# First expert layer of a two-layer attention and expert kernel: another order of the work around the routed tiles, a first batch that enters the feed-forward part in halves, a leaky step on GpSimd

## The reference, cut to what matters

```python
logits = (x @ wt.T + repeat(g @ wg.T)) / 2.0
scores = softmax(logits);  topk_w, topk_idx = top_k(scores, 2);  topk_w /= topk_w.sum(-1)
y_all  = (leaky(x @ w_gate[e]) * (x @ w_up[e])) @ w_down[e]        # only the chosen experts matter
p      = (leaky(x @ sw_gate) * (x @ sw_up)) @ sw_down              # leaky slope 0.01
y      = (y_all[topk_idx] * topk_w).sum(1) + p
# feed-forward part on y:
h = silu(y @ w1.T * s1) * (y @ w2.T * s2)
h = gelu(h @ h1.T * s);  h = gelu(h @ h2.T * s);  x = x + h @ w3.T * s3
```

## Time and profile before

| what | us |
|---|---|
| median of 3 runs | 2638.07 (2637.86 to 2645.0) |
| profiled execution, whole | 2652.06 |
| its span, first to last instruction | 2650.2 |
| TensorE busy in the span | 2507.8 (95%) |
| VectorE busy | 1417.1 (53%) |
| ScalarE busy | 1071.4 (40%) |
| GpSimd busy | 983.2 (37%) |
| mean granted TensorE clock | 0.967 of full |

### The profile page before, as it was taken

One profiled execution on the slowest core, in us unless ns is written; L12 is line 12 of the kernel. 1 busy time (PEld: TensorE's weight loads), 2 busy tenths in 40 slices (PEclk: granted clock), 3 DMA queues, 4 the chain that ended last, 5 costly groups with the idle time before them and its releaser, 6 DMA issues. The chain is left out here.

```text
span 2650.2 us, 37857 instructions
## 1 busy us (share of the span) xinstructions
PE 2507.8 (95%) x13266; PEld 1552.1 (59%) x13266; DVE 1417.1 (53%) x3288; ACT 1071.4 (40%) x2618; POOL 983.2 (37%) x1028
## 2 busy tenths in 40 slices
PE   7999999899999899699999999999999899899998
PEld 4565655534343467387878777556656567544456
DVE  7466575467667353432424243565565578455555
ACT  4767676344544223111111111465666355112122
POOL 3655465178768324531212121765655200000000
PEclk9999999989999889799999999999999999999997
DMA  4000000000000146300000100432333000400000
GB/s 160 1 1 1 1 1 21 9 13 13 13 13 9 39 129 198 125 1 1 1 0 1 43 1 1 146 123 77 106 114 98 0 1 1 131 1 3 3 10 26
DMA packets 91518, 108.52 MB, mean 41 GB/s; under 512 B 16396, under 2 KB 72597, under 8 KB 91078
## 3 DMA queue, kind: packets, MB, share of 16 engines
q1 hardware_dynamic: 87606, 96.27, 11.5%
q0 software_dynamic: 3728, 9.83, 1.3%
HBM read 92.52 MB, written 9.35 MB: 38 GB/s over the span
## 5 line engine op out<-in xcount | busy, mean ns | idle before, releaser
L1014 POOL TENSOR_TENSOR cb_sc<-cb_toep,cb_mk 128x128 f32<-128x128 f32 (+3 forms) x256 | 215.6, 870 | 190.7 <-ACT cb_pr L1052 180.1
L1014 POOL TENSOR_TENSOR cb_bias<-cb_bias,cb_mk 128x128 f32<-128x128 f32 (+3 forms) x256 | 215.3, 871 | 148.6 <-DMA cb_bias<-in_fside_16xSxS 148.5
L1653 DVE TENSOR_REDUCE gb_bmax<-PS 128x8 f32<-128x512 f32 x256 | 164.5, 685 | 87.0 <-PE PS L1431 86.6
L398 PE MATMUL PS<-ident,cb_pr 128*128 128x128 f32 x1280 | 198.6, 284 | 4.0 <-ACT cb_pr L1052 2.3
L699 DVE CUSTOM_DVE_ANT_0 cb_sc<-PS,cb_sc,cb_sneg 128x128 f32<-128x128 f32 (+3 forms) x256 | 129.9, 547 | 125.0 <-PE PS L388 121.5
L398 PEld LDWEIGHTS PS<-ident,cb_pr 128*128 128x128 f32 x1280 | 135.3, 141 | 96.9 <-issue 82.7
L1812 ACT ACTIVATE gb_pt<-PS 128x512 f32<-128x512 f32 x256 | 139.4, 596 | 111.0 <-PE PS L1438 105.8
L1058 ACT ACTIVATE cb_pt<-PS 128x128 f32<-128x128 f32 (+3 forms) x448 | 163.6, 414 | 39.1 <-PE PS L398 38.6
L1431 PE MATMUL PS<-gb_ks,gb_qs 32*128 32x512 f32 x512 | 171.6, 668 | 8.0 <-DVE gb_bmax L1653 6.4
L699 DVE CUSTOM_DVE_ANT_0 cb_bias<-PS,cb_bias,cb_sneg 128x128 f32<-128x128 f32 (+3 forms) x256 | 129.3, 546 | 90.2 <-PE PS L388 89.3
L2347 PE MATMUL PS<-eb_g,ff_h 128*128 128x256 f32 x768 | 175.4, 382 | 0.0
(11 more groups left out here) (652 smaller groups left out, 5039.2 us busy)
## 6 DMA issues: line engine op xcount, KB each, us to landing
cb_bias<-in_fside_16xSxS SPq DMA_DIRECT2D x64, 256.0 KB, 2.9
cb_bias<-in_fside_16xSxS SPq DMA_DIRECT2D x64, 192.0 KB, 2.5
ff_h<-in_L_ffn_h_w SPq DMA_DIRECT2D x2, 4096.0 KB, 15.6
cb_bias<-in_fside_16xSxS SPq DMA_DIRECT2D x64, 128.0 KB, 2.2
y_rows<-eb_g SPq DMA_DIRECT2D x19, 256.0 KB, 2.2
cb_toep<-rel_table SPq DMA_DIRECT2D x8, 512.0 KB, 7.4
cb_bias<-in_fside_16xSxS SPq DMA_DIRECT2D x64, 64.0 KB, 2.2
ff_w<-in_L_ffn_w_w SPq DMA_DIRECT2D x3, 1024.0 KB, 8.3
```

Source lines behind the costliest of these rows:

```text
L398: ins = pe.transpose(PS[:, bank, j * P:j * P + P], pr[:, v % 2, e, j * P:j * P + P], ident)
L1014: ins = pool.tensor_tensor(biases(v, e), turned(h, n) if L0 else biases(v, e), mk[:, b % 2, packed(t):packed(t) + n], ALU.add)
L1653: dve.tensor_reduce(bmax[:, n % 2, t, g + e, 0:NB], PS[:, bank + e, :].rearrange("p (n k) -> p n k", k=64), AX.X, ALU.max)\
```

## The change

In TensorE's order `into(0, 0)` and `into(0, 1)` move between the transposes and logits (and wait for 4 of the 5 shared weight loads; the fifth, `sw_down`, has the semaphore `mo_back`), `into(1, 1)` is split around `ranks`, and `turn_rows(1)` moves behind `pair_into(0)`. The ring `turned` has two banks instead of four, `logit` has banks 6 and 7. VectorE's order moves the products between the routing steps. Leaky of batches 0 to 2 becomes two ScalarE operations (0.01 x and 0.99 relu(x), both from PSUM) and an addition on GpSimd; batch 3 keeps the old form. The second multiplication of `hot_tiles` moves to GpSimd. Small dummy activations of Exp and Silu are added. There are two buffers `yg0` and `yg1` (batch 1 uses `yg1`, in h2's place); the gathers of a batch go by halves (tiles 0, 1 of both experts, then tiles 2, 3); batch 0 and 1 are gathered without a wait between, batch 2 waits for `mo_y` 1, batch 3 for `mo_y` 3 and stands behind the first group of weight sums. Batch 0 is combined, transposed and multiplied with w1 and w2 in two halves of 256 columns; `combine(1)` and `combine(2)` stand behind tiles 2 and 6 of the second half, `combine(3)` behind tile 1 of batch 1. S3 is made in two halves for each step. Cut to its core:

```diff
-        L, Hq, Hd = cut(2 * NJ, P, dtype=BF16), cut(2 * NJ, TILES, dtype=BF16), cut(2 * NJ, 2, TILES, dtype=BF16)
+        yg1, Hq, Hd = cut(YG, D), cut(2 * NJ, TILES, dtype=BF16), cut(2 * NJ, 2, TILES, dtype=BF16)
+        L = flat(yg1).bitcast(BF16).rearrange("p (k m) -> p k m", m=P)
...
+        yg = lambda b: yg1 if b == 1 else yg0
...
-            Turns(sm, uses, k) for k in ((0, 1, 6, 7), (4, 5), (0, 1), (2, 3), (4, 5), (6, 7), (6, 7), (6, 7)))
+            Turns(sm, uses, k) for k in ((0, 1), (6, 7), (0, 1), (2, 3), (4, 5), (6, 7), (6, 7), (6, 7)))
...
-                        pe.wait_ge(sm["mo_shared"], 16 * 5)
-                    for ring, name in ((gates, "gate"), (ups, "up")):
-                        bank = ring.put(pe, (name, b, e))
-                        for c in range(DC):
-                            ins = pe.matmul(PS[:, bank, :], sw[name][:, c, e, :], x_of(b)[:, c, :], start=(c == 0),
-                                            stop=(c == DC - 1))
-                        ins.then_inc(ring.filled((name, b, e)), 1)
+                        pe.wait_ge(sm["mo_shared"], 16 * 4)
+                    into_one(gates, "gate", b, e)
+                    into_one(ups, "up", b, e)
...
+                def turn_first_y(half):
+                    pe.wait_ge(sm["mo_y" if half else "mo_half"], 1)
+                    for c in range(DC):
+                        bank = turned_y.put(pe, (0, c, half))
+                        for e in range(2):
+                            ins = pe.transpose(PS[:, bank, e * P:e * P + P], yr[:, 2 * half + e, c * P:c * P + P], ident)
+                        ins.then_inc(turned_y.filled((0, c, half)), 1)
...
+                def first_hidden(half):
+                    for c in range(DC):
+                        turned_y.wait_emptied(pe, (0, c, half))
+                    if half == 0:
+                        pe.wait_ge(sm["ff_in"], 16 * 6)
+                    for m in range(FC):
+                        if half == 0 and m == 5:
+                            turn_first_y(1)
+                        for ring, name in ((gates, "w1"), (ups, "w2")):
+                            item = (name, 0, m) if half else (name, "half", m)
+                            bank = ring.put(pe, item)
+                            for c in range(DC):
+                                ins = pe.matmul(PS[:, bank, 0:HS], wf[name][:, c, m * P:m * P + P], yT[:, c, half * HS:half * HS + HS],
+                                                start=(c == 0), stop=(c == DC - 1))
+                            ins.then_inc(ring.filled(item), 1)
...
                 turn_x(1, 1)
                 logits(0)
+                into(0, 0)
                 turn_x(2, 0)
                 turn_x(2, 1)
                 logits(1)
+                into(0, 1)
                 turn_x(3, 0)
                 turn_x(3, 1)
                 logits(2)
                 logits(3)
...
-                into(0, 0)
-                into(0, 1)
                 into(1, 0)
                 down(0)
+                into_one(gates, "gate", 1, 1)
                 ranks()
-                into(1, 1)
+                into_one(ups, "up", 1, 1)
...
-                    if i + 1 < PAIRS:
+                    if 1 <= i and i + 1 < PAIRS:
                         turn_rows(i + 1)
                     if i < PAIRS:
                         pair_into(i)
+                    if i == 0:
+                        turn_rows(1)
...
-                turn_y(0)
-                for b in range(B):
+                turn_first_y(0)
+                first_hidden(0)
+                first_hidden(1)
+                feed_forward(0)
+                for b in range(1, B):
+                    hidden(b)
...
-                    link(dve.tensor_tensor(Hq, iota[:, 0:TILES].unsqueeze(1).to_broadcast([P, 2 * NJ, TILES]),
-                                           hi[:, :].unsqueeze(2).to_broadcast([P, 2 * NJ, TILES]), ALU.is_equal))
-                    dve.tensor_scalar(Hd[:, :, 0, :], Hq, own, None, ALU.mult)
-                    link(dve.tensor_tensor(Hd[:, :, 1, :], Hq, column.unsqueeze(2).to_broadcast([P, 2 * NJ, TILES]), ALU.mult))
+                    dve.tensor_tensor(Hq, iota[:, 0:TILES].unsqueeze(1).to_broadcast([P, 2 * NJ, TILES]),
+                                      hi[:, :].unsqueeze(2).to_broadcast([P, 2 * NJ, TILES]), ALU.is_equal).then_inc(sm["mo_tile_hot"], 1)
+                    dve.wait_ge(sm["mo_tile_hot"], 1)
+                    link(dve.tensor_scalar(Hd[:, :, 0, :], Hq, own, None, ALU.mult))
...
+                def gated_half(m, half):
+                    item = lambda name: (name, 0, m) if half else (name, "half", m)
+                    bank = ups.take(dve, item("w2"))
+                    gates.wait_emptied(dve, item("w1"))
+                    dve.scalar_tensor_tensor(out=g1[:, m, half * HS:half * HS + HS], in0=PS[:, bank, 0:HS],
+                                             scalar=wf["w2_s"][:, m:m + 1], in1=sa[:, m % 2, 0:HS], op0=ALU.mult,
+                                             op1=ALU.mult).then_inc(ups.emptied(item("w2")), 1)
...
                 copy_logits(1)
+                products(0, 0)
                 copy_x(3)
...
-                products(0, 1)
                 pick_second()
                 products(1, 0)
                 sums()
                 slots_of_tokens()
+                products(1, 1)
                 hot_tiles()
-                products(1, 1)
                 hot_slots(0)
                 hot_slots(1)
+                products(2, 0)
+                rows_of_slots()
+                products(2, 1)
                 experts_of_tiles()
-                products(2, 0)
-                products(2, 1)
-                rows_of_slots()
                 weights_of_tokens()
                 for i in range(PAIRS + 1):
                     if i < PAIRS:
                         pair_products(i)
                     if i:
                         copy_hidden(i - 1)
-                products(3, 0)
-                products(3, 1)
+                for e in range(2):
+                    leaky(3, e)
+                    products(3, e)
+                combine(0, (0, 1), "mo_half")
+                copy_first_y(0)
+                for m in range(FC):
+                    gated_half(m, 0)
+                    if m == 3:
+                        combine(0, (2, 3), "mo_y")
+                    elif m == 4:
+                        copy_first_y(1)
                 for b in range(B):
                     more = b + 1 < B
-                    if b == 0:
-                        ya.wait_emptied(dve, ("p", B - 1))
-                        yb.wait_emptied(dve, ("p", B - 1))
-                        combine(0)
-                        copy_y(0)
                     for m in range(FC):
-                        gated_rows(b, m)
+                        if b:
+                            gated_rows(b, m)
+                        else:
+                            gated_half(m, 1)
                         if m == 5:
                             first_sums(b, 1, 0)
                             third_sum(b, 1, 0)
-                        if b == 0 and m in (3, 4, 6):
-                            combine({3: 1, 4: 2, 6: 3}[m])
+                        if b == 0 and m == 2:
+                            combine(1, range(NT), "mo_y")
+                        elif b == 0 and m == 6:
+                            combine(2, range(NT), "mo_y")
+                        if b == 1 and m == 1:
+                            combine(3, range(NT), "mo_y")
...
+                        ups.wait_emptied(act, ("up", b - 1, e))
+                    if b < B - 1:
+                        act.activation(lk[:, e, :], PS[:, bank, :], ACT.Copy, scale=0.01)
+                        ins = act.activation(gs[:, e, :], PS[:, bank, :], ACT.Relu, scale=0.99)
+                    else:
+                        ins = act.activation(gs[:, e, :], PS[:, bank, :], ACT.Copy)
+                    ins.then_inc(gates.emptied(("gate", b, e)), 1)
 
...
+                act.activation(warm[:, 0:1], small["first"][:, 0:1], ACT.Exp, scale=0.0)
+                copy_x(0)
+                copy_x(1)
+                copy_x(2)
+                gate_copy(0, 0)
+                copy_x(3)
+                gate_copy(0, 1)
...
+                act.activation(warm[:, 1:2], small["first"][:, 0:1], ACT.Silu, scale=0.0)
...
+                def leaky(b, e):
+                    gates.wait_emptied(pool, ("gate", b, e))
+                    pool.tensor_tensor(lk[:, e, :], lk[:, e, :], gs[:, e, :], ALU.add).then_inc(sm["mo_lk"], 1)
+
+                def return_rows(b):
+                    if b > 1:
+                        pool.wait_ge(sm["mo_y"], b - 1 if b == 2 else b)
+                    for half in range(2):
+                        for k in range(2):
+                            for t in (2 * half, 2 * half + 1):
+                                n, at = k * NT + t, k * NJ + b * NT + t
```

(24 more changed lines are left out.)

89 lines of the change are left out of this document (55 added, 34 removed).

## The result

| | before | after |
|---|---|---|
| median of 13 runs each, us | 2641.41 (2637.26 to 2647.63) | 2626.19 (2616.93 to 2634.71) |
| ratio, 95% interval | | 0.9934 [0.9919, 0.9949] |
| profiled execution, us | 2652.06 | 2626.76 |
| mean granted clock | 0.967 | 0.976 |

The change makes the kernel 17.4 us faster by the ratio (0.66%; the interval is 13.5 to 21.4 us). I had forecast 23.5 us and 2614.6 us; the median lies 2.7 us above the end of my range. The two profiled executions differ by 25.3 us, more than the medians: the profile of before lies 10.7 us above its median, that of after 0.6 us above its own.

What follows compares the result with a forecast made beforehand. TensorE's waits and low clock ahead of 1160 us were taken as the loss. 20.5 us (second part) plus 3.0 (first part) make 23.5, from 2638.07 to 2614.6 us; own range 2609 to 2622, whole range 2600.5 to 2623.5.

Steps and rivals of the forecast that it cites:

- Part two: From the first returning gather to P5 of the first product: 84.4 us become 63.9, 20.5 us won (ends 18 to 25).
- T: Time of the first returning gather, 1046.86 us before the change, from which the feed-forward entry's steps are counted.
- Rival 1: Feed-forward entry: combine(1)'s sums are not held; 8.3 + 2.4 us more won, 2603.9 us; chance 0.18.
- rival 2: Feed-forward entry: DMA engines full with h1, first four gathers no sooner than all eight; 4.6 us less, 2619.2 us; chance 0.10.
- rival 4: Start: GpSimd multiplies element by element, delaying hot_slots and all gathers; at 35 us the time is 2646.7 us; chance 0.03.
- the collision: Second half: combine(1)'s sums held by GpSimd's weight sums; TensorE loses 8.3 us and 2.4 us of clock.
- T2's lead: First group's end: T2, behind combine(2), is ready about 3 us before P6's second half wants it, so costs nothing.
- Part one: Up to the first pair: reordered start brings gathers and pair loop earlier, 3.0 us won (ends minus 1.0 to 6).
- rival 3: Up to the first pair: clock stays low and GpSimd holds routing; minus 1.0 instead of plus 3.0, 2618.6 us; chance 0.08.

Runs made afterwards that it cites:

- b_again: The kernel before, unchanged, run again on another chip: ratio 0.9999 to before.
- c1_early: The kernel after with combine(1) moved behind tile 6 of the first half: ratio 0.9914 to before.
- combine_early: c1_early with combine(2) also moved two tiles earlier, behind tile 4 of the second half: ratio 0.9922 to before.
- after_again: The kernel after, unchanged, on a second chip: ratio 0.9925 to before.
- after_third: The kernel after, unchanged, on a third chip: ratio 0.9945 to before.
- new_start: The kernel after with its new start kept but before's whole entry into the feed-forward part: ratio 1.0001 to before.

## Why the prediction was right or wrong

**Part two, forecast 20.5, measured 21.6 us in the first pair of profiles: right, step by step.** First product at T + 12.3 (12.3 forecast); GpSimd's block at T + 33.6 (34.6); `combine(1)` at T + 34.8 (34.9); four sums held by GpSimd's four operations for 8.8 us and four free behind them; TensorE's gap 7.1 us (8.3); P5 at T + 62.8 (63.9). No wait for S2, `combine(2)` without cost before T2. Rival 1 (no collision), rival 2 (no earlier half batch) and rival 4 (a dear multiplication on GpSimd, 2.28 us) fell. On the other chips the part is 17.2 and 18.0 us against b_again's 83.7, at and below the lower of my ends for it (18), in part as TensorE stood 2 us more in the first half there (last section). c1_early shows the price of the collision: 8.3 + 2.4 us were charged to it, and moving it away gave 7.7 to 8.5 against the profiles of after with the same longer first half. Another 1.6 us are the T2 wait that came up behind it; I had put T2's lead at about 3 us, and it was 1.1 in after.

**Part one, forecast plus 3.0, measured minus 0.6 in the first pair: the step that failed.** It is rival 3 with nearly its number (minus 1.0), in that profile. `pair_into(0)` was to start 4.6 us earlier, counted from the first transpose, and started 0.1 later. Three terms make up these 4.8 us.

1. The clock and the wait ahead of `ranks`, 2.5 us. I had the shared weights landing 5.0 us after the first transpose (924.1) and full clock from 3.6 us behind that until about 941. They landed at 6.1, so TensorE stood for 1.35 us, which I had counted at nothing; the clock, which fell at 922, was low into 928 to 929, 5.3 us behind the start of `into(0, 0)`, and again for 6.8 us up to 946. `ranks` started 34.8 us after the first transpose (33.7 before), where I had 32.3.
2. From `ranks` to the end of the routing rows, 1.2 us: 16.4 for my 15.2. GpSimd's multiplication took 2.28 us, less than my 2.9, but `hot_slots` took 6.51 us with both leaky additions beside it, where I had 1.3 for one of them and 4.5 behind it.
3. From the first gather to `pair_into(0)`, 1.1 us. `down(2)` waited 1.28 us for its product, which stands behind the row numbers in VectorE's order, and then met the low clock (5.35 us in place of 3.69). It ended 5.3 us behind the first gather, where I had 3.6.

On the other chips `ranks` came at 30.9, 1.4 us earlier than I had it, and (2) and (3) were there in the same size. So part one gave 3.3 us at the first gather, 3.6 at `pair_into(0)` and 3.4 at T: that 3.1 and 3.0 were forecast is in part luck, as the errors cancel. The forecast had one value for the low stretches at the start, and fourteen profiles show several; its ends (minus 1.0 to plus 6) did hold both results.

The rule of the Trainium skill that I weighed (page "SBUF — State Buffer", section "Who interferes with whom") is that a `tensor_scalar` can be held by GpSimd too. The trace agrees: the operation of 0.55 us took 2.67 beside GpSimd's 2.28. It ended 0.3 us behind GpSimd's operation. What it cost isn't shown: `hot_slots` has two inputs in SBUF and would probably have been held by the same operation of GpSimd. Operations of VectorE with one input from PSUM kept their 0.48 us beside the same sums, as `gated_half` at 1091.08 beside S1 in combine_early.

**The base, and why the range was missed.** The median lies 11.6 us above my number. 3.3 of them are the base: I took 2638.07 us, a median of three runs, and the thirteen runs give 2641.41. A base of 2641.41 alone, or part one's full 3.0 us alone, would have put the median inside the range. 2.6 us are the sum: from the first transpose to P5 after is 20.9 us shorter in the first pair, not 23.5 (and 20.6 and 21.4 in after_again and after_third against b_again). The other 5.7 us, between these 20.9 and the 15.2 by which the medians differ, are not explained. By the ratios, which use all runs, the gains are 17.4, 19.9 and 14.6 us, each with 4 to 5 us of uncertainty; two of the three intervals hold 21. In the profiles the rest doesn't lie ahead of the first transpose (919.1 and 916.5 for before, 917.4, 919.2 and 919.6 for after) nor surely behind P5, where one kernel spreads over 4 us. That the first profile of before, 14 us above the median that I started from, showed greater losses than a usual execution is not the reason: b_again's profile lies at its median, that of new_start, which has before's entry, 9 us under its own, and T to P5 is 83.7 and 83.4 us there. The executions of after spread from 2616.9 to 2634.7 us, and the shorter ones have the higher mean clock (0.979 to 0.972); where in the kernel that lies, no profile here tells.

## What to carry to other kernels

- When a change moves two-input VectorE work and GpSimd work close to each other, write down the start of both from one common event. Here both starts came out within 1 us of the trace, and the price of the meeting within 1.2 us. What helped was a place with nothing of the kind beside it (`combine(1)` behind the seventh tile of the first half); a wait on GpSimd only moved the meeting.
- Giving idle GpSimd small operations is no gain if VectorE's next operation has two SBUF inputs and is on the path: 1.45 us were taken off VectorE and 2.0 came back in `hot_slots`, and the stretch from `ranks` to the routing rows took 16.4 us with them and 13.7 without.
- A short wait near a change of the clock can come with more than its own length: 1 us of wait went with 6.8 us more at the low level, though in new_start the clock was low for 10.2 us at a stretch with no wait at all. Compare times within a stage, from an event of its own, and over several profiles, before a few us are ascribed to an edit.
- Take the base of a forecast from as many runs as its range is narrow: here three runs and thirteen differ by 3.3 us, and the range was missed by 2.7.

## What the runs showed of the hardware that I had not expected

On the three other chips the engines stand still together in the pair loop, in both kernels. In b_again ("remote" stands where the trace has no instruction that ended the wait):

```profile
985.06 0.95 POOL L2941 DMA_INDIRECT eb_g<-x_rows,eb_row_at  x1 [0.30 <-issue]
988.54 0.38 ACT L2849 ACTIVATE eb_S<-PS 128x256 f32<-128x256 f32 x1 [8.32 <-remote]
...
989.12 1.10 POOL L2941 DMA_INDIRECT eb_g<-x_rows,eb_row_at  x1 [3.11 <-remote]
...
989.99 0.66 PE L2282 MATMUL PS<-ident,eb_S 128*128 128x128 f32 x2 [6.29 <-DVE eb_S L2585]
```

TensorE's row before ended at 983.7, and ScalarE got its signal at 988.5. TensorE's longest gap there is 3 to 7.3 us, 10 to 16 us behind the start of `pair_into(0)`; six of the traces have one of 1.6 to 2.3 us ahead of it. The loop up to T takes 74.4 to 79.1 us from `pair_into(0)` in these traces, 68.7 and 69.2 in the first two. The kernels with part two have more idle TensorE there in the first half of the first batch too, 1 to 3 us (2.93 in one gap in after_again, no such gap in the first profile of after). A packet of the queue that the profile's page calls instruction starts at 983.8 in b_again, but one does so at 986.1 in the first profile of before too, where nothing halts. The cause was not tried and stays open.
